# Both routers of a graph and expert network: tokens stationary, eight gate columns moving, on one core

## The reference

```python
def _L0_ffn_ref(h, gate_w, gate_b, w1, b1, w2, b2):
    x = h.reshape(T, D)
    logits = x @ gate_w + gate_b            # (T, 256) @ (256, 8) + (8,)
    probs = softmax(logits)
    idx = argmax(probs); prb = probs[idx]
    ...                                     # places in each expert's buffer, relu(x w1 + b1) w2 + b2
def _L1_ffn_ref(x, gate_w, gate_b, W1, b1, W2, b2):
    logits = xf @ gate_w + gate_b           # the same shapes
    probs = softmax(logits)
    top2_vals, top2_idx = top_k(probs, 2)
    ...                                     # gelu(x W1 + b1) W2 + b2, weighted with top2_vals
x = x + _L0_gnn_ref(layernorm(x), ...)
x = x + _L0_ffn_ref(layernorm(x), ...)
x = x + _L1_gnn_ref(layernorm(x), ...)
x = x + _L1_ffn_ref(layernorm(x), ...)
```

## Time and profile before

| | |
|---|---|
| median of 3 runs | 2569.36 us (2565.12 to 2570.14) |
| profiled execution | 2576.82 us, its span 2575.1 us |
| TensorE busy | 2261.5 us, 88% of the span |
| VectorE busy | 1991.4 us, 77% |
| ScalarE busy | 1436.9 us, 56% |
| GpSimd busy | 1550.1 us, 60% |
| mean granted TensorE clock | 0.928 of full speed |

### The profile page before, as it was taken

How to read it: one execution, slowest core, us unless ns; L and a number is a source line. 1 busy time by engine, 2 the same in 40 slices (tenths; PEclk the granted TensorE clock), 3 DMA queues, 4 the chain that set the end, 5 groups by cost and what they waited for, 6 DMA issues and landing times. The chain is left out here.

```text
span 2575.1 us, 61409 instructions
## 1 busy us (share of the span) xinstructions
PE 2261.5 (88%) x16596; PEld 1888.3 (73%) x16596; DVE 1991.4 (77%) x7342; ACT 1436.9 (56%) x4584; POOL 1550.1 (60%) x1544
## 2 busy tenths in 40 slices
PE   5785878999987699967999999999999998749993
PEld 3674546886664366655999999999999997728993
DVE  8885799999886544354899999999999997574334
ACT  0783003444442122235888888888888887623441
POOL 1235777777774477444677777777777773505541
PEclk9897588999997799988999999999999999869997
DMA  5313333434434245422233333333333343052224
GB/s 178 113 32 98 100 96 99 104 102 101 106 106 132 82 147 176 148 74 76 71 80 77 80 79 77 80 78 79 79 78 80 88 77 71 1 198 75 71 71 166
DMA packets 245577, 246.34 MB, mean 96 GB/s; under 512 B 142916, under 2 KB 202335, under 8 KB 244996
## 3 DMA queue, kind: packets, MB, share of 16 engines
q0 software_dynamic: 57344, 151.11, 21.3%
q1 hardware_dynamic: 184596, 88.07, 12.4%
q10 hardware_dynamic: 3312, 3.28, 0.4%
HBM read 189.82 MB, written 52.50 MB: 94 GB/s over the span
## 5 line engine op out<-in xcount | busy, mean ns | idle before, releaser
L2361 POOL DMA_INDIRECT l_rows<-xl_tab,l_ra x454 | 451.4, 994 | 140.7 <-issue 100.1
L1031 POOL DMA_INDIRECT room_a<-h_tab,c_rec x432 | 439.0, 1016 | 138.1 <-issue 76.9
L1078 PE MATMUL c_ps<-room_a 128*128 128x256 f32 x864 | 309.6, 448 | 83.7 <-DVE room_a L1360 45.7
L2369 POOL TENSOR_TENSOR l_low<-l_rest 128x520 bf16<-128x520 f32 x227 | 239.3, 1054 | 142.6 <-DVE l_rest L2515 141.2
L1048 ACT ACTIVATE s_cum<-iota_f,c_row_f 128x128 f32<-128x128 f32 x391 | 122.8, 389 | 311.3 <-PE c_ps_s L1116 205.0
L1078 PEld LDWEIGHTS c_ps<-room_a 128*128 128x128 f32 x864 | 160.2, 210 | 182.6 <-DVE room_a L1360 127.3
L2408 ACT ACTIVATE l_val<-l_rows,l_val 128x64 f32<-128x64 f32 x908 | 241.6, 337 | 7.4
L2433 PE MATMUL l_bank_l<-g_att_d,l_rz 128*128 128x4 f32 x1816 | 242.9, 254 | 0.4 <-ACT l_rz L2420 0.3
L2398 ACT ACTIVATE room_a<-room_a,l_cexp x908 | 241.4, 345 | 1.1 <-issue 1.0
L2477 PE MATMUL l_ps_lb<-ident,l_ls 128*128 128x128 f32 x1816 | 237.2, 274 | 0.6 <-DVE l_ls L2539 0.6
L1116 PE MATMUL c_ps_s<-s_cum 128*128 128x272 f32 x782 | 230.3, 392 | 0.0
(11 more groups left out here) (632 smaller groups left out, 6065.5 us busy)
## 6 DMA issues: line engine op xcount, KB each, us to landing
m_w<-in_L_ffn_w SPq DMA_DIRECT2D x16, 1024.0 KB, 6.8
rec_a<-room_a SPq DMA_DIRECT2D x114, 102.0 KB
l_ra<-rec_a SPq DMA_DIRECT2D x227, 51.0 KB, 2.4
e_w<-in_L_ffn_W SPq DMA_DIRECT2D x16, 512.0 KB, 12.1
l_rows<-xl_tab,l_ra POOLq DMA_INDIRECT x454
room_a<-h_tab,c_rec POOLq DMA_INDIRECT x432, 2.8
e_w<-ye_buf SPq DMA_DIRECT2D x4, 1280.0 KB, 10.5
yd_buf<-m_clean SPq DMA_DIRECT2D x7, 512.0 KB, 10.9
```

The costliest lines, as they stand in the source:

```text
L1031: pool.indirect_dma_start(rows[:, u, :], None, K["h_tab"], bass.IndirectOffsetOnAxis(ap=rec[:, n % RSLOTS, k, 0:1].bitcast(I32), axis=0)). ...
L1078: pe.matmul(ps[s % NB][:, :], hot[:, u, :], rows[:, s % RU, :], start=True, stop=True).then_inc(s_agg, 1)
L2361: pool.indirect_dma_start(rows[:, u, j, :], None, K["xl_tab"], bass.IndirectOffsetOnAxis(ap=ra[:, u, j, A_SRC:A_SRC + 1].bitcast(I32), axi ...
L2369: pool.tensor_tensor(low[:, r % 2, :], rest[:, r % 2, :], uppers(rest[:, r % 2, :]), ALU.subtract).then_inc(S["low"], 1)
```

## The change

In both routers the operands of the gate's multiplication trade places. The turned tile (128 features x 128 tokens of `xt`) becomes the stationary operand and the gate's 128 x 8 half moves, twice for each tile (the two halves of D), so the result already has tokens on partitions and goes straight into the PSUM bank from which `lg` is made. `lt`, its semaphores, the turning back and the additions of the bias by quad are gone. The bias is loaded to all 128 partitions and added once, in the instruction that moved the logits to `lg`. The second router's diff is the same with its own names.

```diff
-        gate_b = t("gate_b", [EXP0, 1], F32)
+        gate_b = t("gate_b", [P, EXP0], F32)
...
-        lt = xint[0:EXP0, :, :]
...
-            sp.dma_start(gate_b[:, :], a["L0_ffn_gate_b"].rearrange("(e o) -> e o", o=1)).then_inc(s_small, 16)
+            sp.dma_start(gate_b[:, :], a["L0_ffn_gate_b"].partition_broadcast(P)).then_inc(s_small, 16)
...
-            for g in range(len(QUADS) + 3):
+            for g in range(len(QUADS) + 1):
...
-                if 1 <= g <= len(QUADS):
+                if g >= 1:
                     v = g - 1
-                    n = len(QUADS[v]) * P
                     pe.wait_ge(s_xtc, 2 * v + 2)
-                    wait(pe, s_lt, v - 1)
-                    for k in range(2):
-                        mm = pe.matmul(ps_y[v % 2][0:EXP0, 0:n], gate[:, k, :], xt[:, v % 2, k, 0:n],
-                                       start=(k == 0), stop=(k == 1))
+                    for j, tile in enumerate(QUADS[v]):
+                        for k in range(2):
+                            mm = pe.matmul(ps_t[:, tile * EXP0:(tile + 1) * EXP0], xt[:, v % 2, k, j * P:(j + 1) * P],
+                                           gate[:, k, :], start=(k == 0), stop=(k == 1))
                     mm.then_inc(s_lp, 1)
-                if g >= 3:
-                    v = g - 3
-                    pe.wait_ge(s_lt, v + 1)
-                    for j, tile in enumerate(QUADS[v]):
-                        mm = pe.transpose(ps_t[:, tile * EXP0:(tile + 1) * EXP0], lt[:, v % 2, j * P:(j + 1) * P],
-                                          ident[0:EXP0, 0:EXP0])
-                    mm.then_inc(s_back, 1)
...
-            for g in range(len(QUADS) + 2):
-                if g < len(QUADS):
-                    wait(dve, s_xt, g - 1)
-                    wait(dve, s_xnst[g % 2], 16 * (g // 2))
-                    for tile in QUADS[g]:
-                        normal(tile).then_inc(s_xn, 1)
-                if g >= 2:
-                    v = g - 2
-                    n = len(QUADS[v]) * P
-                    if v == 0:
-                        dve.wait_ge(s_small, 64)
-                    dve.wait_ge(s_lp, v + 1)
-                    wait(dve, s_back, v - 1)
-                    dve.tensor_scalar(lt[:, v % 2, 0:n], ps_y[v % 2][0:EXP0, 0:n], gate_b[:, :], None, ALU.add
-                                      ).then_inc(s_lt, 1)
-            dve.wait_ge(s_back, len(QUADS))
-            o.did(dve.tensor_copy(lg[:, :, :].rearrange("p t e -> p (t e)"), ps_t[:, :]))
+            for g in range(len(QUADS)):
+                wait(dve, s_xt, g - 1)
+                wait(dve, s_xnst[g % 2], 16 * (g // 2))
+                for tile in QUADS[g]:
+                    normal(tile).then_inc(s_xn, 1)
+            dve.wait_ge(s_small, 64)
+            dve.wait_ge(s_lp, len(QUADS))
+            o.did(dve.tensor_tensor(lg[:, :, :], ps_t[:, :].rearrange("p (t e) -> p t e", e=EXP0),
+                                    gate_b[:, :].rearrange("p (o e) -> p o e", o=1).to_broadcast([P, NT, EXP0]), ALU.add))
```

More of the change, by code:

```diff
@@ L1456, in experts_top1 @@
             sem("m_" + n) for n in ("dve", "var", "std", "xn", "xt", "xtc", "lp", "lg"))
-        s_b2, s_rows, s_lt, s_back = (sem("m_" + n) for n in ("b2", "rows", "lt", "back"))
+        s_b2, s_rows = (sem("m_" + n) for n in ("b2", "rows"))
         s_shift, s_exp, s_hot, s_rank, s_b1, s_b1t = (
@@ L2888, in experts_top2 @@
             t(n, [P, NT], F32) for n in ("tmp", "rstd", "best", "den", "valid", "away"))
-        gate, gate_b = t("gate", [P, 2, EXP1], F32), t("gate_b", [EXP1, 1], F32)
+        gate, gate_b = t("gate", [P, 2, EXP1], F32), t("gate_b", [P, EXP1], F32)
         rev, iota_t = t("rev", [P, EXP1], F32), t("iota_t", [P, NTOP2], F32)
@@ L2894, in experts_top2 @@
         xt = t("xt", [P, 2, 2, QUAD * P], F32)
-        lt = t("lt", [EXP1, 2, QUAD * P], F32)
         lg, ex, one1, one2 = (t(n, [P, NT, EXP1], F32) for n in ("lg", "ex", "one1", "one2"))
@@ L2930, in experts_top2 @@
         ps_y = [c.enter_context(nc.psum_tensor(f"e_ps_y{k}", [P, 512], F32)) for k in range(2)]
-        s_small, s_const, s_dve, s_std, s_xn, s_xt, s_xtc, s_lp, s_lt, s_back = (
-            sem("e_" + n) for n in ("small", "const", "dve", "std", "xn", "xt", "xtc", "lp", "lt", "back"))
+        s_small, s_const, s_dve, s_std, s_xn, s_xt, s_xtc, s_lp = (
+            sem("e_" + n) for n in ("small", "const", "dve", "std", "xn", "xt", "xtc", "lp"))
         s_shift, s_exp, s_hot, s_rank, s_lg = (sem("e_" + n) for n in ("shift", "exp", "hot", "rank", "lg"))
@@ L2959, in _ @@
             sp.dma_start(gate[:, :, :], a["L1_ffn_gate_w"].rearrange("(k p) e -> p k e", p=P)).then_inc(s_small, 16)
-            sp.dma_start(gate_b[:, :], a["L1_ffn_gate_b"].rearrange("(e o) -> e o", o=1)).then_inc(s_small, 16)
+            sp.dma_start(gate_b[:, :], a["L1_ffn_gate_b"].partition_broadcast(P)).then_inc(s_small, 16)
             sp.dma_start(b1_rows[:, :], a["L1_ffn_b1"].rearrange("e (f p) -> (e f) p", p=P)).then_inc(s_b1_rows, 16)
@@ L3067, in _ @@
                     mm.then_inc(s_xt, 1)
-                if 1 <= g <= len(QUADS):
+                if g >= 1:
                     v = g - 1
-                    n = len(QUADS[v]) * P
                     pe.wait_ge(s_xtc, 2 * v + 2)
[L3072 to L3075, removed]
+                    for j, tile in enumerate(QUADS[v]):
+                        for k in range(2):
+                            mm = pe.matmul(ps_l[:, tile * EXP1:(tile + 1) * EXP1], xt[:, v % 2, k, j * P:(j + 1) * P],
+                                           gate[:, k, :], start=(k == 0), stop=(k == 1))
                     mm.then_inc(s_lp, 1)
[L3077 to L3083, removed]
             pe.wait_ge(s_xtc, 2 * len(QUADS))
@@ L3143, in _ @@
             dve.wait_ge(s_small, 32)
[L3144 to L3149, removed]
             def per_token(v):
@@ L3156, in _ @@
             revb = rev[:, :].rearrange("p (o e) -> p o e", o=1).to_broadcast([P, NT, EXP1])
-            dve.wait_ge(s_back, len(QUADS))
-            o.did(dve.tensor_copy(lg[:, :, :].rearrange("p t e -> p (t e)"), ps_l[:, 0:NT * EXP1]))
+            dve.wait_ge(s_lp, len(QUADS))
+            o.did(dve.tensor_tensor(lg[:, :, :], ps_l[:, 0:NT * EXP1].rearrange("p (t e) -> p t e", e=EXP1),
+                                    gate_b[:, :].rearrange("p (o e) -> p o e", o=1).to_broadcast([P, NT, EXP1]), ALU.add))
             o.then()
```

## The result

The changed kernel takes 2578.96 us (median of 13 runs, 2573.11 to 2587.10) against 2566.64 us for the kernel before (13 runs, 2560.75 to 2572.63): ratio 1.0050, 95% interval 1.0038 to 1.0061. It is 12.3 us slower. The forecast had the direction and most of the mechanism, and was too high: 2590.5, with a range down to 2582.

A forecast was written before the change was run, and what follows sets the result against it. TensorE was taken to bound both routers up to the logits. At 1.2 GHz each would take 33.0 us, +9.8 and +11.3, together +21.1 on 2569.36: 2590.5 us, range 2582 to 2596.

The forecast's parts named there:

- The chain, the beat and the prices at 2.4 GHz: In the routers TensorE sets the time; a quad takes 3.17 us now, new pairs 112 ns, saving 0.36 us a quad.
- rival C: In both routers the clock rises as now and stays: −2.6 us each, sum −5.2; chance 0.09.
- VectorE, ScalarE, the bias load, the experts' weights: In and behind both routers, bias additions, copies, the larger bias load and earlier weight landing were taken to change 0 us.
- The clock: TensorE runs at 1.2 GHz in both routers, first to last: +21.1 us; chance 0.47.
- B: A router's clock rises but doesn't last, giving back 3 us: +18.1 with one such router, +15.1 with both; chance 0.37.
- The sum at 1.2 GHz: Each router: 50 transposes 10.8 us, 100 pairs 21.3, changes between them 0.8, the end 0.1; 33.0 us.
- The changes of kind: On TensorE in each router, 11 switches between transposes and pairs at 0.07 us, together 0.8 us.
- The base: Differences were added to the kernel before's median of three runs, 2569.36 us, not to the profiled 2576.82.
- The range's low end: Whole kernel: a short rise in both routers, 2584.5 us, less 2.5 for the spread of runs, gives 2582.
- D: In both routers a pair takes 112 ns at either clock: −0.3 and +1.2 us, together +0.9; chance 0.03.

The follow-up runs named there:

- the kernel with 128 columns: Changed kernel with each pair moving 128 columns, the gate's eight repeated sixteen times, in place of 8: ratio to the kernel before 0.9972.
- single-router kernels: Two kernels, each with the change in only one router and the other left as before: ratio to the kernel before 1.0024 each.
- fillers: 512-column multiplications of ones, results unused, behind each quad's pairs but the last in the changed kernel; two a quad: ratio 0.9984 with warm start, 1.0009 without.

## Why the prediction was wrong

*The chain, the beat and the prices at 2.4 GHz* held. Each microsecond of a router was one of the kernel. A pair, put at 112 ns at 1.00, takes 107 with 8 moving columns, 108 with 64 and 112 with 128. The 0.11 us of a transpose in rival C came from no row (the earlier trace rows give 0.13, eight in 1.02 us); the kernel with 128 columns has 0.109. *VectorE, ScalarE, the bias load, the experts' weights* were put at nothing and cost nothing: the bias once by itself gives ratio 1.0006 with 1 inside its interval, and the stretch from the logits to the first transposes of the experts kept its length to 0.1 us in both single-router kernels.

*The clock: "So I take 1.2 GHz for both routers, first to last."* This is the step that failed. That the narrow pairs run at 1.2 GHz for most of a router is right, and the two kernels that change only the moving columns show that it is the narrow move that does it. But the clock comes up behind the opening transposes more often than I allowed: both times in the changed kernel, once in the two new routers of the single-router kernels, and in twelve of the eighteen routers of all profiles that were entered at 0.50, within 3.5 us. Those are seven of eight second routers and five of ten first ones. (One of the eighteen stood at 1.00 for its first 0.1 us.) I had given it a quarter for each router. The case that occurred in the profile, B in both routers, had a chance of 0.05. Its size for a rise was right: 3 us forecast, 31.61 − 28.48 = 3.1 measured.

*The sum at 1.2 GHz* was mis-sized as well: 33.0 us a router against 31.61 measured where the clock never rose. Pairs take 204 ns between transposes and not 213, 0.9 us in all. The changes of kind, put at 0.8, add nothing: the 204 and the 0.217 of a transpose are read from start to start and have them in, and the 1.74 and 3.27 they come from fill the 5.01 us of a quad. Transposes and the end took 0.3 more than I had put.

Together: 21.1 less twice 1.4 for the sum and twice 3.1 for the rises is 12.1, which is what the two routers of the profile show and 0.2 from the measured difference. With the right sum and no rise it would have been 18.3. That it comes within 0.2 is in part luck: it sets single executions beside medians, and in the three profiles in which the old order entered at 0.50 its first router took 21.7 to 23.2 us and its second 21.7 to 22.2, by when the clock rose.

*The base* moved too. I added to 2569.36 us, a median of three runs; the thirteen give 2566.64. So 2.7 of the 11.5 us between forecast and result have nothing to do with the change. The range's low end, 2582, missed by 3.0 us. It had taken the rises at 3 us and the sum as sure, with no allowance downward; on the right base it would have been 2579.3, and still above the 2578.96 measured.

*The rivals.* B, for both routers, is what the profile shows. C (stays at 1.00) occurred in no profile with 8 moving columns and no fillers; with 64 and 128 it did, and the kernel was 8 to 9 us faster than before. D is refuted: the same sixteen pairs took 1.69 us at 1.00 and 3.21 at 0.50. On the Trainium skill: its "PE-mode transpose" ("TensorE: Matmul & The Clock Gate") says that for transposes the full clock doesn't engage, as they don't count as busy in the same way. The profile above, where the clock rises behind fifteen or sixteen transposes in both routers, disagrees. By the Trainium skill's account on the same page that the clock follows how busy TensorE is ("The HAM clock gate") it should have stayed up; 21.6 us with TensorE's row busy throughout were at 0.50, so the trace disagrees here too.

What stays open: why two fillers held the clock in one router and lost it in the other, why the clock came up behind the opening in some routers and not in others, and how often an unfilled router gets its rise outside the profiled executions. The thirteen runs of the changed kernel lie between 2573 and 2587 us and the profiled one, 2576.78, is in their faster half, so that others had fewer or shorter rises is possible and not shown.

## What to carry to other kernels

Trading a wide moving operand for a narrow one can save time at the full clock and still lose, if the clock stays low under it: look at the granted clock of stretches that resemble the new code before adding up durations at the clock of the old. Where the pace of the pairs hardly depends on the moving columns, as here with a 128 x 128 f32 stationary operand, widening the moving operand costs next to no time (107 ns a pair with 8 columns, 112 with 128) and here went with a clock of 2.4 GHz, which turned a loss of 12 us into a gain of 8. When a forecast hangs on whether the clock rises, count in how many of the comparable places of the trace it did, and let the range cover both answers for each. A warm start made of a fixed number of multiplications is over sooner when the clock is already up, so its end has to reach the work behind it at either clock.

## What the runs showed of the hardware

A PE row at 100% and a PEld row at 100% say nothing of the clock: 31.5 us in a row with 31.50 and 31.48 us busy ran at 0.50. With 8 moving columns a pair takes 204 ns at 0.50 and 107 at 1.00. Two multiplications of ones a quad, whose results are not used, made a router 7 us shorter where they held the clock (19.48 against 26.44 us, both entered at 1.00) and 7 us longer where they didn't (33.28). And 51 multiplications of ones in TensorE's idle time between the logits and the experts of both stages went with a median 4.7 us lower, of five runs each.
